# Two answers of a planned side computation moved to later slots on VectorE (fused attention and FP4 feed-forward, one core)

## What is computed

```python
xn = layernorm(x)                                  # x: (4, 2048, 256)
# attention with linear cost; q, k, v: 256 x 256 weights
Q = l2(xn @ Wq.T + bq);  K = l2(xn @ Wk.T + bk);  V = xn @ Wv.T + bv
tailor = 1 / (256 + Q . (sum of K + 1e-6))
s = xn + gamma * (sum(V) + Q @ (K.T @ V)) * tailor
# feed-forward with blockwise FP4 quantisation of both operands (blocks of 16)
h = silu(q4(xn) @ q4(w_gate).T) * (q4(xn) @ q4(w_up).T)       # 704 wide
g = silu(q4(h) @ q4(w_down).T)
out = x + s * g
```

## Time and profile before

| | before |
|---|---|
| median of 3 runs | 613.37 us (612.94 to 616.39) |
| the profiled execution's own time | 613.37 us |
| its span, first to last instruction | 611.5 us |
| PE busy | 552.4 us, 90% |
| DVE busy | 564.3 us, 92% |
| ACT busy | 411.1 us, 67% |
| POOL busy | 244.3 us, 40% |
| DMA, mean over the span | 48 GB/s |

### The profile page before, as it was taken

One profiled execution on the slowest core, in us unless ns is written; L12 is line 12 of the kernel. 1 busy time (PEld: TensorE's weight loads), 2 busy tenths in 40 slices (PEclk: granted clock), 3 DMA queues, 4 the chain that ended last, 5 costly groups with the idle time before them and its releaser, 6 DMA issues. The chain is left out here.

```text
span 611.5 us, 15155 instructions
## 1 busy us (share of the span) xinstructions
PE 552.4 (90%) x4957; PEld 427.9 (70%) x4957; DVE 564.3 (92%) x1195; ACT 411.1 (67%) x884; POOL 244.3 (40%) x208
## 2 busy tenths in 40 slices
PE   0365889999999999999999989999999999999896
PEld 0243567777787777768887766778787777778775
DVE  6979899999999999999999996999999999977863
ACT  3565778887787777767776766777777777645421
POOL 4442334333343344344443343443343444423236
PEclk9969899999999999999999999999999999999989
DMA  7000000010001101110111111011111111023033
GB/s 245 17 30 23 8 12 21 16 35 11 9 18 36 36 18 54 53 35 28 47 53 54 53 56 55 20 34 54 53 53 53 54 36 35 36 72 119 2 121 139
DMA packets 17473, 29.15 MB, mean 48 GB/s; under 512 B 2672, under 2 KB 4848, under 8 KB 17392
## 3 DMA queue, kind: packets, MB, share of 16 engines
q1 hardware_dynamic: 17392, 28.13, 13.6%
HBM read 19.73 MB, written 8.39 MB: 46 GB/s over the span
## 5 line engine op out<-in xcount | busy, mean ns | idle before, releaser
L1350 PE MATMUL GU<-wgu,xqT 128*128 128x352 f16 x1536 | 255.5, 317 | 7.7 <-DVE h L855 4.7
L1350 PEld LDWEIGHTS GU<-wgu,xqT 128*128 128x128 f16 x1536 | 149.1, 100 | 83.6 <-issue 8.1
L521 POOL TENSOR_TENSOR ht<-h,hrr 128x1408 f32<-128x1408 f32 x32 | 82.9, 2590 | 86.0 <-DVE hrr L869 84.5
L602 ACT ACTIVATE sil<-GU,wkap 128x352 f32<-128x352 f32 x128 | 70.8, 553 | 59.4 <-PE GU L1350 58.3
L1360 PE MATMUL DS<-wdT,hqT 128*128 128x256 f16 x704 | 87.6, 273 | 1.9 <-ACT hqT L609 1.9
L855 DVE SCALAR_TENSOR_TENSOR h<-GU,wkap,sil 128x352 f32<-128x352 f32 x128 | 68.8, 537 | 12.4 <-ACT sil L602 9.2
L903 DVE TENSOR_TENSOR hq<-hg,hs 128x704 f16<-128x704 f16 x128 | 78.3, 652 | 1.0
L487 POOL TENSOR_TENSOR xnat<-xs,xnat 128x510 f16<-128x510 f32 (+1 forms) x32 | 37.1, 1158 | 98.3 <-DVE hq L903 96.4
L1360 PEld LDWEIGHTS DS<-wdT,hqT 128*128 128x128 f16 x704 | 66.7, 98 | 12.1 <-ACT hqT L609 2.3
L477 POOL TENSOR_TENSOR rs<-ve,half 128x2 f32<-128x2 f32 x32 | 25.2, 788 | 122.5 <-DVE ht L892 108.5
L638 ACT ACTIVATE gring<-DS,hun 128x256 f32<-128x256 f32 (+1 forms) x64 | 29.9, 467 | 44.6 <-issue 30.5
(11 more groups left out here) (156 smaller groups left out, 953.8 us busy)
## 6 DMA issues: line engine op xcount, KB each, us to landing
xin<-in_L_attn_x SPq DMA_DIRECT2D x34, 256.0 KB, 2.9
xe<-in_L_attn_x SPq DMA_DIRECT2D x25, 256.0 KB, 2.7
out<-o SPq DMA_DIRECT2D x25, 256.0 KB, 2.1
algebra<-in_L_ffn_w_down SPq DMA_DIRECT2D x1, 704.0 KB, 6.9
gring<-in_L_ffn_w_gate SPq DMA_DIRECT2D x1, 640.0 KB, 4.6
gring<-in_L_ffn_w_up SPq DMA_DIRECT2D x1, 640.0 KB, 5.3
xs<-in_L_attn_x SPq DMA_DIRECT2D x2, 256.0 KB, 4.5
xt<-in_L_attn_x SPq DMA_DIRECT2D x2, 256.0 KB, 4.9
```

Source lines behind the costliest of these rows:

```text
L521: g.tensor_tensor(paired(ht[:, 0:2 * I]), paired(h[:, q]), spread(hrr[:, q], 4 * CB), ALU.mult).then_inc(S["ht_d"], 1)
L602: a.activation(sil[:, c], GU[:, c, 0, 0:CH], ACT.Silu, scale=wkap[:, 0:1]).then_inc(S["sil_d"], 1)
L1350: last = t.matmul(GU[:, c, m, 0:CH], xqT[:, k, j, 2 * a_ + kc], wgu[:, b_, kc, 2 * m + c], start=(z == 0 and kc == 0), stop=(z == 2 and kc ...
```

## The change

Two entries of the table `ANSWERS` get other keys. `gram0` goes from (0, 0, 3) to (0, 1, 0), and `top` from (4, 1, 2) to (5, 0, 0). No instruction is added, removed or changed, PE's, ACT's, POOL's and SP's orders are what they were, and the last batch keeps its own tables.

```diff
-        ANSWERS = {(-4, 1, 1): "own_basis", (0, 0, 3): "gram0", (1, 0, 1): "gram1", (1, 1, 0): "turn", (2, 1, 0): "squares",
-                   (3, 0, 0): "norms", (4, 0, 0): "tailor", (4, 0, 3): "scale", (4, 1, 0): "product", (4, 1, 2): "top", (5, 0, 2): "high_low"}
+        ANSWERS = {(-4, 1, 1): "own_basis", (0, 1, 0): "gram0", (1, 0, 1): "gram1", (1, 1, 0): "turn", (2, 1, 0): "squares",
+                   (3, 0, 0): "norms", (4, 0, 0): "tailor", (4, 0, 3): "scale", (4, 1, 0): "product", (5, 0, 0): "top", (5, 0, 2): "high_low"}
```

## The result

| | before | both moves |
|---|---|---|
| median of 9 runs | 613.55 us | 618.9 us (617.84 to 620.51) |
| ratio | | 1.0078, interval 1.0054 to 1.0101 |
| span of the profiled execution | 611.5 us | 617.7 us |
| PE busy, DVE busy | 552.4, 564.3 us | 553.6, 565.4 us |

What follows compares the result with a forecast made beforehand. DVE was taken to set the pace, with PE holding about 2 us reserve per pass. 613.37 plus 2.65 (0.65 + 1.2 + 0.8) for `gram0` plus 0 for `top` gave 616.0 us, range 613.4 to 619.3.

Steps and rivals of the forecast that it cites:

- rival 1: Clock falls once or twice behind PE's new idle times at `gram1_0`: 617.6 us, or 619.2 with two; chance 0.32.
- What bounds: Over a pass DVE sets the pace; PE, also full, has about 2 us reserve, not available everywhere.
- Where the cost comes in: PE waits at L1420 (`gram1_0`) three times; DVE then waits for `silu` near 285 to 295 and 427 to 435 us.
- Size of the wait: New PE idle ahead of L1420: about 0.5, 2.1 and 1.8 us in the three passes.
- part 2: `top` later: PE waits 0.87 us for `kap` at `high_low`, replacing its wait for the new M; counted 0.
- Part 1 in pass 1: `gram0` later makes PE 0.65 us late at `gram1_0`; all of it reaches DVE: 0.65 us.
- Part 1 in passes 2 and 3 without the clock: `gram0` later: PE 2.5 and 2.1 us late; after returns at `turn` and from reserve, 1.2 and 0.8 us reach DVE.
- the reserve at the closest place: Where `silu` and `h_mul` are closest, at 292.85 us in pass 2, the finished half lies ready 0.6 us; likewise pass 3.
- The clock: Behind new PE idle of 2.1 and 1.8 us, taken as not falling; 1.6 us per fall, 0 to 3.2 in range.
- The shared port: L835, slowed beside POOL's output sum, could regain 0.6 us if DVE stalls before it; counted as changing nothing.
- Rival 2: PE's reserve absorbs passes 2 and 3, pass 1 costs up to 0.65 us: 613.4 to 614.0 us; chance 0.14.
- Rival 4: Faster: L935 fills the 0.1 us gap behind L895, POOL and ACT run ahead; 612.5 us at best; chance 0.05.

Runs made afterwards that it cites:

- the long filler: Kernel with both moves plus 18 unused matmuls on PE ahead of its wait at `gram1_0` in passes 2 and 3; 618.04 us, ratio 1.0063 against before.

## Why the prediction was right or wrong, point by point

The way and the place were right, and the time is in the range; but the forecast itself, 616.0 with no clock fall, was 2.9 us short. What happened is rival 1 with two falls. That its 619.2 lies within 0.3 us of the median is in part luck: by the passes the loss is 7.2 us where that rival has 5.85, and a tail that is 1.6 us shorter in some executions may be what makes up for it.

- **What bounds.** Right: DVE at full, PE with a reserve. The kernels with `gram0` two thirds of the way and with PE's side one slot later show the reserve: PE idle 1.0 to 1.2 us in pass 2, cost 0.05. The window that was read for it, 210 to 334 us, leaves out the slots of `top` and `high_low`; from 253 to 350 us it is the same picture, PE 95.2 and DVE 95.9 of 97 us.
- **Where the cost comes in.** Right: `gram1_0` in all three passes, no wait left at `turn` in passes 2 and 3, and `h_mul` waiting for `silu` at 291 and 297, 434 and 440 us. It also waits at 270.60 and 274.49, and at the same places of pass 3, which was not named; these go with the clock fall. With the long filler only one wait of 0.3 us is left there, in each pass.
- **Size of the wait.** Too small. Said were 0.5, 2.1 and 1.8 us of idle; it was 0.75, 2.56 and 2.10. Two steps failed. PE's start after L939's end was taken as 0.05 us, from `turn`; at L1420 it is 264.48 to 264.70, 0.22. And 0.1 to 0.3 us were taken off because PE would come late out of part 2; it does not, by 253 us PE's and DVE's starts are late by the same 1.63.
- **Part 1 in pass 1**, 0.65 us said, 0.89 with `gram0` alone. All of the lateness went through, as said; the difference is that later start. The place where it comes in was another one. DVE takes 0.3 us of it up to 160 us in small steps, and 0.6 us at L892 (161.50 in the profile after), which now waits for ACT's L651; ACT's copies are late with PE, by the same 0.89 us. In the trace before, L651 ended at 159.97 and this L892 began at 160.00, so the reserve there was 0.03 us.
- **Part 1 in passes 2 and 3 without the clock**, 1.2 and 0.8 us said. The long filler shows 1.65 and 1.62, of which about 0.2 belong to `top`: 1.45 and 1.4. The terms that were mis-sized are the later start, 0.17 us in each pass, and the reserve at the closest place: PE's 4.84 us of shift in pass 2 left 4.46 on DVE, 0.4 taken and not 0.6. Of these 0.2 us, 0.1 is that an `h_mul` that had to wait takes 0.50 us to the next L914 and not 0.40 (297.21 to 297.71, against 292.85 to 293.25). In pass 3 a third part came: the first eight L1420 take 1.80 to 1.88 us at full clock in place of 1.46, and the next eight 1.46 in place of 1.56, so about 0.3 us. In pass 2 the next eight took 1.82 before and 1.46 after, so there it cancels. The parts come to a little more than the difference in pass 2, 0.37 against 0.25; what gave back the rest was not followed.
- **Part 2**, 0 said. Right within what the times tell, 1.0007; by the passes 0.12 to 0.22 us. The wait at L1484 was 0.85 us in pass 2, 0.87 said. The step that had 0.1 us left over, on PE alone, named the wrong engine: it is on DVE.
- **The clock.** This is the step that moved the result. It was taken as not falling, though slightly so, with 1.6 us each as the price. It fell in both passes in each profile of both moves and of `gram0` alone. The price was near: 1.2 to 1.4 us by the passes, 1.6 said. The step that failed behind it is to read the fall from the length of the idle time alone, with 1.73 and 2.23 us as its marks. At the turn of the hardware loop two of the kernels above have an idle time of 2.17 us each ahead of the same matmuls, first `top` alone, then `gram0` alone with PE's side moved, each with the window behind it:

```profile
366.99 1.96 PE L1350 MATMUL GU<-wgu,xqT 128*128 128x352 f16 x12 [2.17 <-issue]
367.90:371.30 3.40, 3.40 (x36) 2.58 (x34) 3.33 (x5) 3.15 (x6) 1.45 (x2) 1.00 0.01 2
...
367.40 3.29 PE L1350 MATMUL GU<-wgu,xqT 128*128 128x352 f16 x12 [2.17 <-issue]
367.90:371.30 3.40, 3.40 (x18) 2.08 (x17) 3.35 (x5) 1.79 (x4) 1.87 (x2) 0.50 0.00 0
```

So an idle time sized right, 2.56 us in place of 2.1, would have made a fall likelier but not certain: with `gram0` two thirds of the way one of 2.31 us left the clock at full. Nor is 1.6 us, or 1.2, the price everywhere. Across the loop's turn, from the `h_mul` behind `high_low` to the one ahead of the next `gram0`, DVE's starts move by +0.01 to -0.23 us against the kernel before, whether the clock falls there or not: where it does not fall, PE stands still for 1.7 to 2.2 us some 10 us later, and where it falls, that wait is 0.4 us or less.

- **The shared port.** L835 behind the DVE stall of pass 2 took 0.97 in place of 1.28 us. It ended 0.55 us after POOL's L537 in both executions (289.33 to 289.88 before, 292.81 to 293.36 after), and only its start came later against it. So it came partly clear, as the lock of the Trainium skill's page "SBUF — State Buffer", section "Who interferes with whom", would have it. As the text said, nothing came of it: the next `h_mul` waited for `silu` all the same.
- **Rival 2**, the reserve takes it all, is what happens at a wait of 1.0 us and not at 2.1. **Rival 4**, faster by the gap behind L895, was tested by the kernel with PE's side moved: the gap of 0.1 us is used (L935 starts 1.53 us after L895), and nothing is gained.

With the passes' measured costs, the forecast would have been 613.4 + 0.9 + 2.7 + 2.9 + 0.5 for `top` = 620.4 us. The measured median is 1.5 us under that, about the size of the fall in the tail that one profile of both moves has and the other has not. That this accounts for the spread of the runs was not tried.

## What to carry to other kernels

A slack between two full engines is a number for each place, not a share: measure how long each result lies ready before its reader comes, and a delay under that number is free, while one over it costs the excess. Here a wait of 1.0 us was free in pass 2, one of 2.1 us and more was not, and one of 0.75 us in pass 1, where no result lay ready, cost 0.9 us. When an answer must move later, look who asks for it, and move the question too; a late answer cost 0.8% with its question in the old slot and nothing that could be measured with the question one slot later. And price the clock with a new idle time of TensorE: here the clock's part was 2.6 of 6.9 us, and keeping PE at useless work recovered it. A trace of one execution does not settle whether the clock falls behind an idle time of about 2 us, so count it as a chance and not as a threshold.

## What the runs showed of the hardware that was not expected

- The length of an idle time of PE of about 2 us does not decide alone whether the clock falls behind it. Idle times of 1.91, 2.10, 2.17, 2.19, 2.23, 2.33, 2.39 and 2.56 us were followed by 3.4 us at 0.50. Others of 1.45, 1.73, 2.00, 2.04, 2.15, 2.17 and 2.31 us were not, those of 2 us and more all at the turn of the hardware loop or 10 us behind it. At `gram1_0` of pass 3 2.10 us was followed by a fall in each of three profiles. What else decides, these runs do not tell.
- The same fall costs 1.2 to 1.4 us behind `gram1_0` in passes 2 and 3, 1.6 us in the tail, and nothing that shows at the turn of the loop.
- Eight matmuls of L1420 in the hardware loop took 1.46 us in some places and 1.80 to 1.88 us in others, at full clock: before, 1.46 at 260.35 and 1.82 at 264.54, neither behind a wait of its own. Where the first eight came late, it was they that took 1.80 to 1.88 and the next eight 1.46. In pass 1, which is written out, all took 1.46, behind a wait of 0.75 us too. A group in the loop computes its operands' addresses from registers between the matmuls; that this is the reason was not tried.
- PE's start after the end of the DVE instruction that it waits for was 0.05 us at the fp32 transposes of `turn` and 0.21 to 0.26 us at the fp16 matmuls of `gram1_0`.
